# A graph, attention and gated-delta layer on one core: three sums leave TensorE, the gate projections move behind the others

## Chip, cores and metric

The kernel runs on 1 core of a Trainium2 chip (TRN2). The metric is the device time of one execution in microseconds (us). Engines are called PE (TensorE matmul), PEld (its weight load), DVE (VectorE), ACT (ScalarE), POOL (GpSimd) and SP (the engine that issues most DMAs).

## What is computed

One layer over 1250 nodes with 512 features, all in float32. Cut to what matters here:

```python
xn  = layernorm(x)
# graph convolution over 20000 edges plus self loops
deg = segment_sum(ones, dst_with_loops)          # edges into each node, plus 1
agg = segment_sum((xn @ W)[src] * (deg**-0.5)[src] * (deg**-0.5)[dst], dst)
# linear attention, 8 heads of 64
Q, K, V = elu(xn@Wq.T+bq)+1, elu(xn@Wk.T+bk)+1, xn@Wv.T+bv
mix = (Q @ (K^T V)) / (Q . K.sum(nodes) + 1e-6) @ Wo.T + bo
x   = x + relu(agg + b) + mix
# feed-forward: top-2 of 4 memories, gated delta rule, 8 heads of 64
h = layernorm(x)
q, k, v = l2norm(silu(h@Wq)), l2norm(silu(h@Wk)), silu(h@Wv)
beta, g = sigmoid(h@Wb), -exp(A_log)*softplus(h@Wa+dt_bias)
core = recurrence(q, k, v, beta, g)              # per memory and head
out  = x + (rmsnorm(core) * o_norm_weight * silu(h@Wg)) @ Wo
```

## The kernel before

Everything is scheduled by hand: each engine has one written list of instructions, and counting semaphores (`S[...]`) order the engines among themselves. An engine works strictly in the order of its list. Nodes are cut into NT = 10 tiles `t` of P = 125 rows; the 512 features into KC = 4 pieces `k` or `c` of 128. The stages, in the order of PE's list:

1. **Transposes** of the normalised rows into `xT`.
2. **Key and value stage** (PE lines L489 to L544). For each tile: four key matmuls (`project`, with the bias as a one-row matmul, L487), four value matmuls, and `kv_sums` (L538), which adds K^T V into PSUM bank 4 (L542) and the column sums of K into bank 5 with a column of ones (L544). From tile 2 on, 16 "sort steps" (L496) are put between them: small f16 matmuls that sort the edges into cells. DVE builds their one-hot operands in groups of four (`sort_four`, L1396 to L1400) and writes the finished key tile `tC` (L1413).
3. **Query and mixing stage** (L575, L596, L518, L520). `mix(t, b0)` makes one tile of the mixing output: a one-row bias matmul (L518) and four matmuls (L520). DVE adds the result to `x_all` (`mix_out`, L1441). Tiles 0 to 7 are made here, tiles 8 and 9 after the counting.
4. **Counting stage**. In NB = 20 groups `g` of SC = 9 steps, PE multiplies one-hot rows of sources with one-hot rows of destinations (`count_step`, L505), which gives the matrix `cnt` of edge counts; ACT copies it out of PSUM (L1020). DVE builds the one-hots: `oh_src` once a group (L1484), `oh_dst` once a step into WB = 4 buffers (L1488). Two of the matmuls of `xn @ W` (L653) stand in each group. POOL adds the unit matrix to the diagonal blocks of `cnt` (L1169), and after every second group PE sums the columns of the finished tile of `cnt` with ten one-column matmuls (`degrees`, L509 to L511). At the end DVE copies the degrees (L1530), POOL raises them to the power -0.5 (L1171, `dinv`), and DVE scales the rows `hs` (L1547).
5. **Aggregation** (L716): `cnt` times `hs`, 100 pairs.
6. **Feed-forward projections** (L748). `project_rows(t, w)` makes tile t of projection w (0 q, 1 k, 2 v, 3 gate), four matmuls each. ACT applies Silu (L1063, L1066). For q and k, DVE sums squares (`squares`, L1657), POOL takes the power (`inverse_norm`, L1185), DVE scales (`unit_rows`, L1665, L1667) and POOL scatters the finished row tile to `qkv_slots` in HBM with two indirect DMAs (`rows_out`, L1190). `gates_out` (L1180) scatters decays and betas; SP reads them back as `gbp`; `gates_in` on DVE orders them; `decay_sums` on PE (L760 to L767), `decays` on ACT (L1043) and `decay_rows` on DVE turn them into decay rows, which SP stores and loads again (L397, L404). SP then loads the sorted q and k rows (`load_qk`, L420).
7. **Chunk recurrence** in ten rounds: `features` transposes q and k (L794), `key_key` is the first of its products (L782), and so on.
8. **Output**: gather, norm, gate, last matmul (L958), store.

The order of the loops of stage 6, and where the decay work stands in them, is set by hand: by the loop over `w` and by `GAMMA_AT`. The code touched by the change:

## Time and profile before

| | before |
|---|---|
| median of 3 runs | 1128.72 us (1125.96 to 1130.7) |
| the profiled execution | 1125.21 us |
| its span | 1123.3 us |
| PE busy | 962.7 us (86%) |
| DVE busy | 598.7 us (53%) |
| POOL busy | 337.2 us (30%) |
| ACT busy | 249.0 us (22%) |
| mean granted TensorE clock | 0.948 of full speed |

The span is the stretch from the first to the last profiled instruction, and the execution's own time is 1.91 us more. Busy shares say which engine has most to do over the whole, not which one is waited for in a stage. The mean clock is that which the chip granted to PE over the span.

### The profile page before, as it was taken

The page shows a single profiled execution, that of the slowest core. Times are in us where ns is not written, and L with a number is a line of the kernel's source. Part 1 is how long each engine was busy: PE and PEld are TensorE (multiplying, and loading weights), DVE is VectorE, ACT ScalarE, POOL GpSimd, SP SyncE. Part 2 cuts the span into 40 slices and gives each one's busy share as a digit, 9 for nine tenths or more (in the row PEclk, how much of TensorE's full clock was granted, in tenths as well). Part 3 has the DMA queues.
Part 4 walks back from the last instruction along what each step waited for, and adds up shares of the span by engine and source line. Part 5 has one row for each costly group of instructions (what it writes and reads, how often), then busy time and mean ns, then how long its engine had stood idle before and what let it go on. Part 6 is the DMA issues. An engine that isn't in the chain of part 4 may idle for free.

```text
span 1123.3 us, 28924 instructions
## 1 busy us (share of the span) xinstructions
PE 962.7 (86%) x12841; PEld 620.7 (55%) x12841; DVE 598.7 (53%) x1297; ACT 249.0 (22%) x497; POOL 337.2 (30%) x284
## 2 busy tenths in 40 slices
PE   0899999999999989988999956878788987888468
PEld 0444444343777734434444426878778877788333
DVE  7878885333777522224533334555555644554265
ACT  0211112100111100003111113324423342233142
POOL 4000000000010000000585346554645464544282
PEclk9899999979999989998999987999999989999879
DMA  9100000000000041000044255443344334422252
GB/s 295 41 1 1 1 1 0 1 0 1 1 1 1 1 157 49 1 0 1 3 171 125 113 206 158 104 108 78 98 113 124 86 86 116 116 68 51 58 159 83
DMA packets 69982, 77.96 MB, mean 69 GB/s; under 512 B 33665, under 2 KB 55323, under 8 KB 69855
## 3 DMA queue, kind: packets, MB, share of 16 engines
q1 hardware_dynamic: 64735, 54.94, 18.1%
q0 software_dynamic: 5120, 21.14, 5.4%
q8 instruction: 103, 1.69, 0.6%
q14 instruction: 24, 0.20, 0.1%
HBM read 51.70 MB, written 24.35 MB: 68 GB/s over the span
## 4 chain that ended last, share of the span: by engine, by line
PE 80%; issue 6%; DVE 6%; ACT 3%; POOL 2%; DMA 1%; SPq 1%; ACTq 0%; DVEq 0%; POOLq 0%
PE bank L782 14%; PE bank L748 12%; PE bank L716 8%; PE bank L489 6%; PE bank L505 4%; PE bank L520 3%; PE bank L958 3%; PE bank L653 3%; PE bank L575 2%; PE bank L883 2%; PE bank L496 2%; PE bank L511 2%; PE bank L872 2%; PE bank L859 2%; PE bank L893 2%
## 5 line engine op out<-in xcount | busy, mean ns | idle before, releaser
L748 PE MATMUL bank<-W,xT 128*128 128x512 f32 x320 | 137.8, 593 | 0.0
L1169 POOL TENSOR_TENSOR big<-big,ident_sb 125x125 f32<-125x125 f32 x10 | 9.9, 989 | 346.2 <-ACT big L1020 346.2
L748 PEld LDWEIGHTS bank<-W,xT 128*128 128x128 f32 x320 | 60.6, 190 | 75.6 <-issue 75.6
L716 PE MATMUL bank<-hs,big 125*125 125x512 f32 x200 | 86.7, 593 | 1.3 <-DVE hs L1547 1.3
L1720 DVE TENSOR_TENSOR tB<-bank,masks_sb 128x512 f16<-128x512 f32 x80 | 52.7, 687 | 59.0 <-PE bank L782 58.8
L489 PE MATMUL bank<-W,xT 128*125 128x512 f32 x160 | 81.8, 610 | 0.0
L1488 DVE TENSOR_SCALAR rows<-iota_sb,tC 128x625 f16<-128x625 f16 x180 | 58.1, 383 | 30.6 <-PE bank L505 30.1
L782 PE MATMUL bank<-tB 64*64 64x64 f16 x2560 | 56.7, 200 | 15.7 <-issue 9.1
L505 PEld LDWEIGHTS bank<-rows 128*125 128x125 f16 x360 | 48.4, 144 | 31.2 <-issue 20.5
L505 PE MATMUL bank<-rows 128*125 128x313 f16 x360 | 62.4, 313 | 2.6 <-DVE rows L1488 2.4
L716 PEld LDWEIGHTS bank<-hs,big 125*125 125x125 f32 x200 | 37.2, 188 | 49.3 <-issue 48.5
L782 PEld LDWEIGHTS bank<-tB 64*64 64x64 f16 x2560 | 52.4, 116 | 19.0 <-issue 16.6
L782 PE MATMUL bank<-big 64*64 64x64 f32 x1920 | 59.1, 219 | 0.0
L782 PEld LDWEIGHTS bank<-big 64*64 64x64 f32 x1920 | 58.1, 135 | 0.3 <-issue 0.3
L1084 ACT ACTIVATE tA<-bank 128x512 f16<-128x512 f32 x60 | 36.0, 600 | 90.4 <-PE bank L782 90.3
L1220 POOL TENSOR_TENSOR big<-state,gtot 128x256 f32<-128x256 f32 x40 | 24.5, 612 | 101.0 <-DVE state L1748 101.0
L782 PE MATMUL bank<-tA 64*64 64x64 f16 x1280 | 34.1, 200 | 23.6 <-issue 20.5
L1398 DVE TENSOR_SCALAR rows<-iota_sb,gbp 125x180 f16<-125x180 f16 x160 | 51.5, 322 | 0.0
L1400 DVE TENSOR_SCALAR rows<-iota_sb,gbp 125x180 f16<-125x180 f16 x160 | 51.3, 321 | 0.0
L1162 POOL TENSOR_TENSOR rstd<-mv,phalf 125x5 f32<-125x5 f32 (+2 forms) x5 | 11.7, 2343 | 128.9 <-DVE mv L1316 128.9
L1227 POOL TENSOR_TENSOR tB<-tA,masks_sb 128x512 f16<-128x512 f16 x20 | 26.7, 1352 | 70.6 <-DVE tA L1705 70.6
L489 PEld LDWEIGHTS bank<-W,xT 128*125 128x125 f32 x160 | 28.0, 191 | 34.1 <-issue 34.1
(286 smaller groups left out, 1902.6 us busy)
## 6 DMA issues: line engine op xcount, KB each, us to landing
big<-qkv_slots SPq DMA_DIRECT2D x20, 512.0 KB, 5.4
rows<-step_rows SPq DMA_DIRECT2D x40, 128.0 KB, 3.8
rows<-gam_rows SPq DMA_DIRECT2D x40, 128.0 KB, 3.3
big<-qkv_slots SPq DMA_DIRECT2D x80, 64.0 KB, 3.9
big<-qkv_slots SPq DMA_DIRECT2D x40, 128.0 KB, 2.8
o_slots<-big SPq DMA_DIRECT2D x40, 128.0 KB, 2.4
x_all<-in_x SPq DMA_DIRECT2D x10, 224.0 KB
out<-tC SPq DMA_DIRECT2D x10, 224.0 KB
```

What stands on the lines that cost most here:

```text
L489: last = mm(dst, xT[:, k, t * P:(t + 1) * P], W[:, w, k, :], start=(k == 0 and bias is None), stop=(k == KC - 1))
L505: last = mm(bank[0:P, b0 + k, 0:n], oh_src[:, g % 2, j, 0:P], oh_dst[:, i % WB, t0:t0 + n], start=(j == 0), stop=(j == SC - 1))
L520: last = mm(bank[0:P, b0, :], qs[g % 2][:, c, at:at + P], W[:, 3, c, :], start=False, stop=(c == KC - 1))
L653: last = mm(bank[0:P, 6, :], xT[:, k, s * P:(s + 1) * P], W[:, 4, k, :], start=(k == 0), stop=(k == KC - 1))
L716: last = mm(bank[0:P, t % 2, :], cnt[:, s, t * P:(t + 1) * P], hs[:, s, :], start=(s == 0), stop=(s == NT - 1))
L748: last = mm(bank[:, 2 + w, :], xT[:, k, t * P:t * P + 128], W[:, w, k, :], start=(k == 0), stop=(k == KC - 1))
L782: last = mm(bank[q, b0, a * CL:(a + 1) * CL], lhsT[q, a, :], rhs[q, a, :], start=True, stop=True)
L1084: A(flat(T0[s] if lv == LEVELS - 1 else T16[s]), bank[:, TB[s], :], ACT.Copy).then_inc(S["t_done"], 1)
L1398: V.tensor_scalar(oh_col[:, i % (2 * SB), 0, :], iota[0:P, 0:SW], e_col[:, i:i + 1], e_src[:, i:i + 1], ALU.is_equal, ALU.mult)
L1400: V.tensor_scalar(oh_col[:, i % (2 * SB), 1, :], iota[0:P, 0:SW], e_col[:, i:i + 1], e_dst[:, i:i + 1], ALU.is_equal, ALU.mult).then_inc(S ...
L1488: V.tensor_scalar(oh_dst[:, i % WB, :], iota[:, 0:HN], srt[:, 1, i:i + 1], None, ALU.is_equal).then_inc(S["onehots_done"], 1)
L1720: V.tensor_tensor(B16[s], pm(MB[s]), bm(level[lv], 8), ALU.mult).then_inc(S["b_done"], 1)
```

## The change

Four things are changed, none of them in what is computed.

- **Mixing bias.** The one-row matmul L518 in `mix` goes. `bo` is loaded into all 125 rows, and POOL adds it to `x_all` ten times ahead of `mix_out`.
- **Key sums.** The ones-column matmul L544 goes from `kv_sums`. POOL adds the ten key tiles into `k_sum`; one ones-column matmul and four one-column matmuls on `k_sum` follow after the last `kv_sums`.
- **Degrees.** `oh_src` gets a 126th column of ones, so that row 125 of each product holds the counts per destination. Ten SP DMAs bring these rows to `deg_rows`, ten one-column matmuls turn them into columns, and DVE adds 1 for the loop. The 100 matmuls of `degrees` remain only in a branch for edge lists that need a second round. Edge destinations carry an offset of 1 so that empty places match no column. `mix(8)` and `mix(9)` now stand ahead of the degrees and the branch, and the feed-forward weights are loaded after `deg_psum`.
- **Gate projections.** `project_rows(t, 3)` moves behind all tiles of the other three; `project_rows(1, 0)` moves ahead of the routing matmuls; `decay_sums`, `decays` and `decay_rows` move up to tile 8, `gates_in` to tile 7, and DVE's `gate_rows` move behind the first `decay_matrix` pair.

```diff
@@ -49,7 +49,8 @@
 GB_FIRST = 4
-GAMMA_AT = 6
+GAMMA_AT = 7
+DECAY_AT = 8
@@ -147,7 +148,8 @@
         rows_all = sb("rows", [128, 6 * D])
-        b_o = xn[0:1, 0, :]
+        b_o = xn[0:P, 0, :]
+        k_sum = tA[0:P, 0, :]
@@ -172,6 +174,7 @@
+        deg_rows = W[0:NT, 1, :, :].rearrange("p k n -> p (k n)")[:, 0:N]
@@ -322,6 +325,14 @@
             return (LEVELS - 1) * (u - u % 2) + 2 * (lv - 1) + u % 2 + 1
+
+        def feature_count(t, w):
+
+            return 3 * NT + t + 1 if w == 3 else 3 * t + w + 1
+
+        def feature_bank(t, w):
+
+            return (5, 2, 3, 4)[t % 4] if w == 3 else 2 + w
@@ -373,8 +384,12 @@
             sp.wait_ge(S["kv_psum"], NT)
-            sp.dma_start(b_o, d["L0_mix_bo"].unsqueeze(0)).then_inc(S["bias_loaded"], 16)
+            sp.dma_start(b_o, d["L0_mix_bo"].partition_broadcast(P)).then_inc(S["bias_loaded"], 16)
+            for s in range(NT):
+                sp.wait_ge(S["count_done"], 2 * s + 2)
+                sp.dma_start(deg_rows[s:s + 1, :], big[P:OW, s * N:(s + 1) * N]).then_inc(S["deg_rows_loaded"], 16)
             sp.wait_ge(S["mix_psum"], NT)
+            sp.wait_ge(S["deg_psum"], 1)
@@ -502,7 +517,7 @@
                 for k, (t0, n) in enumerate(HCOLS):
-                    last = mm(bank[0:P, b0 + k, 0:n], oh_src[:, g % 2, j, 0:P], oh_dst[:, i % WB, t0:t0 + n],
+                    last = mm(bank[0:OW, b0 + k, 0:n], oh_src[:, g % 2, j, :], oh_dst[:, i % WB, t0:t0 + n],
@@ -515,9 +530,8 @@
                 at = (t - SEGS[g][0]) * P
-                mm(bank[0:P, b0, :], ones[0:1, 0:P], b_o, start=True, stop=False)
                 for c in range(KC):
-                    last = mm(bank[0:P, b0, :], qs[g % 2][:, c, at:at + P], W[:, 3, c, :], start=False, stop=(c == KC - 1))
+                    last = mm(bank[0:P, b0, :], qs[g % 2][:, c, at:at + P], W[:, 3, c, :], start=(c == 0), stop=(c == KC - 1))
@@ -532,17 +546,15 @@
             pe.wait_ge(S["off_done"], 2)
-            mm(bank[:, 5, :], zeros16[:, 0:128], zeros16[:, :], start=True, stop=True)
...
                 for c in range(KC):
-                    mm(bank[:, 4, c * 128:(c + 1) * 128], xn[0:P, t % 2, c * 128:(c + 1) * 128],
+                    last = mm(bank[:, 4, c * 128:(c + 1) * 128], xn[0:P, t % 2, c * 128:(c + 1) * 128],
                        tC[0:P, t % 2, c * 128:(c + 1) * 128], start=False, stop=True, skip_group_check=True)
-                mm(bank[0:1, 5, :], ones[0:P, 0:1], tC[0:P, t % 2, :], start=False, stop=True,
-                   skip_group_check=True).then_inc(S["kv_psum"], 1)
+                last.then_inc(S["kv_psum"], 1)
@@ -604,13 +616,16 @@
             kv_sums(NT - 1)
+            pe.wait_ge(S["pool_added"], NT - 1)
+            mm(bank[0:1, 5, :], ones[0:P, 0:1], k_sum, start=True, stop=True)
+            for c in range(KC):
+                last = mm(bank[:, 6, c:c + 1], k_sum[:, c * 128:(c + 1) * 128], ones[0:P, 0:1], start=True, stop=True)
+            last.then_inc(S["kv_psum"], 1)
...
             for c in range(KC):
-                mm(bank[:, 4, c * 128:(c + 1) * 128], b_v[:, c * 128:(c + 1) * 128], ks_row[:, c * 128:(c + 1) * 128],
+                last = mm(bank[:, 4, c * 128:(c + 1) * 128], b_v[:, c * 128:(c + 1) * 128], ks_row[:, c * 128:(c + 1) * 128],
                    start=False, stop=True, skip_group_check=True)
-            for c in range(KC):
-                last = mm(bank[:, 6, c:c + 1], ks_row[:, c * 128:(c + 1) * 128], ones[0:1, 0:1], start=True, stop=True)
@@ -653,11 +667,6 @@
                             last.then_inc(S["h_psum"], 1)
-                if g % 2 == 0 and g >= 2:
-                    pe.wait_ge(S["loops_added"], s)
-                    degrees(s - 1)
-            pe.wait_ge(S["loops_added"], NT)
-            degrees(NT - 1).then_inc(S["deg_psum"], 1)
@@ -678,22 +687,28 @@
+            pe.wait_ge(S["count_done"], NB)
+            for t in (8, 9):
+                mix(t, 2 + t % 2)
+            pe.wait_ge(S["h_done"], NT)
+            pe.wait_ge(S["deg_rows_loaded"], 16 * NT)
+            for t in range(NT):
+                last = mm(bank[0:P, 6, t:t + 1], deg_rows[:, t * P:(t + 1) * P], ones[0:NT, 0:1], start=True, stop=True)
+            last.then_inc(S["deg_psum"], 1)
+
             pe.wait_ge(S["rounds_done"], 1)
...
             with pe.If(n_rounds > 1):
-                pe.wait_ge(S["counted"], 1)
+                pe.wait_ge(S["mix_done"], NT)
                 with pe.Fori(1, n_rounds) as r:
...
                     count_round(r)
-                pe.wait_ge(S["counted"], 2)
+                pe.wait_ge(S["counted"], 1)
                 mm(bank[:, 7, 0:16], zeros16[:, 0:128], zeros16[:, 0:16], start=True, stop=True)
-            pe.wait_ge(S["count_done"], NB)
-            for t in (8, 9):
-                mix(t, 2 + t % 2)
             pe.wait_ge(S["h_done"], NT)
@@ -742,15 +757,21 @@
             def project_rows(t, w):
-                if t:
-                    pe.wait_ge(S["f_act"], 4 * (t - 1) + w + 1)
+                b0 = feature_bank(t, w)
+                if w < 3 and t:
+                    pe.wait_ge(S["f_act"], feature_count(t - 1, w))
+                if w == 3 and 1 <= t < 4:
+                    pe.wait_ge(S["f_act"], feature_count(NT - 1, t - 1))
+                if w == 3 and t >= 4:
+                    pe.wait_ge(S["f_act"], feature_count(t - 4, 3))
                 for k in range(KC):
-                    last = mm(bank[:, 2 + w, :], xT[:, k, t * P:t * P + 128], W[:, w, k, :], start=(k == 0), stop=(k == KC - 1))
+                    last = mm(bank[:, b0, :], xT[:, k, t * P:t * P + 128], W[:, w, k, :], start=(k == 0), stop=(k == KC - 1))
-            for w in range(4):
+            for w in range(3):
...
                 project_rows(0, w)
+            project_rows(1, 0)
@@ -767,9 +788,13 @@
             for t in range(1, NT):
-                for w in range(4):
+                for w in range(1 if t == 1 else 0, 3):
                     project_rows(t, w)
-            decay_sums()
+                if t == DECAY_AT:
+                    decay_sums()
+            pe.wait_ge(W_loaded[3], 32)
+            for t in range(NT):
+                project_rows(t, 3)
@@ -1163,6 +1196,14 @@
             rstd_of(2)
+            for t in range(1, NT):
+                pool.wait_ge(S["k_done"], t + 1)
+                if t >= 2:
+                    pool.wait_ge(S["pool_added"], t - 1)
+                G.tensor_tensor(k_sum, tC[0:P, 0, :] if t == 1 else k_sum, tC[0:P, t % 2, :], ALU.add).then_inc(S["pool_added"], 1)
+            pool.wait_ge(S["bias_loaded"], 32)
+            for t in range(NT):
+                G.tensor_tensor(x_all[:, t, :], x_all[:, t, :], b_o, ALU.add).then_inc(S["pool_added"], 1)
@@ -1334,11 +1375,11 @@
             step(V.tensor_scalar(e_int, e_int, 1, None, ALU.arith_shift_right))
-            step(V.tensor_copy(e_dst, e_int))
+            step(V.tensor_scalar(e_dst, e_int, 1.0, None, ALU.add))
...
             for b in range(NB):
-                step(V.tensor_scalar(binm[:, b, :], e_bin, float(b), None, ALU.is_equal))
+                step(V.tensor_scalar(binm[:, b, :], e_bin, float(b - 2), None, ALU.is_equal))
@@ -1410,6 +1451,7 @@
                     dve.wait_ge(S["kv_psum"], t - 1)
+                    dve.wait_ge(S["pool_added"], max(t - 2, 1))
@@ -1437,6 +1479,7 @@
             def mix_out(t, b0):
+                dve.wait_ge(S["pool_added"], NT + t)
@@ -1473,15 +1516,16 @@
                 dve.wait_ge(S["sort_used"], r * EPP + EPP)
-                V.tensor_scalar(srt[:, 0, :], bank[:, 7, 0:SW], -1.0, None, ALU.add).then_inc(S["sorted"], 1)
-                V.tensor_copy(srt[:, 1, :], bank[:, 7, SW:2 * SW]).then_inc(S["sorted"], 1)
+                V.tensor_scalar(srt[:, :, :], bank[:, 7, 0:2 * SW].rearrange("p (a n) -> p a n", a=2), -1.0, None,
+                                ALU.add).then_inc(S["sorted"], 1)
             keep_sorted(0)
-            dve.wait_ge(S["sorted"], 2)
+            dve.wait_ge(S["sorted"], 1)
+            V.memset(oh_src[:, :, :, P:OW], 1.0)
...
                     dve.wait_ge(S["onehots_used"], (g - 1) * SC)
-                V.tensor_tensor(oh_src[:, g % 2, :, :], bm(iota[:, 0:OW], SC), bc(srt[:, 0, g * SC:(g + 1) * SC], OW), ALU.is_equal)
+                V.tensor_tensor(oh_src[:, g % 2, :, 0:P], bm(iota[:, 0:P], SC), bc(srt[:, 0, g * SC:(g + 1) * SC], P), ALU.is_equal)
@@ -1526,8 +1570,10 @@
+            mix_out(8, 2)
+            mix_out(9, 3)
             dve.wait_ge(S["deg_psum"], 1)
-            V.tensor_copy(deg[:, :], bank[0:P, 7, 0:NT]).then_inc(S["counted"], 1)
+            step(V.tensor_scalar(deg[:, :], bank[0:P, 6, 0:NT], 1.0, None, ALU.add))
@@ -1538,8 +1584,6 @@
             V.tensor_copy(n_r, n_max).then_inc(S["deg_final"], 1)
-            mix_out(8, 2)
-            mix_out(9, 3)
@@ -1675,11 +1719,9 @@
                 unit_rows(t)
-                if t:
-                    gate_rows(t - 1)
...
                     gates_in()
-                if t == NT - 2:
+                if t == DECAY_AT:
@@ -1757,6 +1799,8 @@
             both(decay_matrix, 0)
+            for t in range(NT):
+                gate_rows(t)
```

Three places in the order of instructions (a row is source line, operation, output and inputs, shape, and how many in a row; the line numbers after the change are those of the new file, about 15 to 20 higher). First, PE in the middle of the counting stage, around the end of a second group, before:

```order
L653 MATMUL bank<-W,xT 125x512
L505 MATMUL bank<-rows 125x313
L505 MATMUL bank<-rows 125x312
L511 MATMUL bank<-ones,big 125x1 x10
L505 MATMUL bank<-rows 125x313
L505 MATMUL bank<-rows 125x312
```

and now:

```order
L667 MATMUL bank<-W,xT 125x512
L520 MATMUL bank<-rows 126x313
L520 MATMUL bank<-rows 126x312
L520 MATMUL bank<-rows 126x313
L520 MATMUL bank<-rows 126x312
L520 MATMUL bank<-rows 126x313
```

The ten one-column matmuls between two groups are gone, and a count matmul has 126 output rows in place of 125. Second, PE at the end of the counting, before (the branch body, which does not run with these inputs, is left out at the "..."):

```order
L505 MATMUL bank<-rows 125x313
L505 MATMUL bank<-rows 125x312
L511 MATMUL bank<-ones,big 125x1 x10
L682 TENSOR_LOAD rounds
...
L518 MATMUL bank<-xn,ones 125x512
L520 MATMUL bank<-W 125x512 x4
L518 MATMUL bank<-xn,ones 125x512
L520 MATMUL bank<-W 125x512 x4
L716 MATMUL bank<-hs,big 125x512 x60
```

and now:

```order
L520 MATMUL bank<-rows 126x313
L520 MATMUL bank<-rows 126x312
L534 MATMUL bank<-W 125x512 x8
L696 MATMUL bank<-ones,W 125x1 x10
L700 TENSOR_LOAD rounds
...
L731 MATMUL bank<-hs,big 125x512 x60
```

The last two mixing tiles moved ahead of the degrees, so the degrees, the register load and the branch now stand directly ahead of the aggregation. Third, PE in the feed-forward projections, before:

```order
L748 MATMUL bank<-W,xT 128x512 x16
L756 MATMUL bank<-sel,lt_sb 125x40
L757 MATMUL bank<-sel,onesq 125x40
L748 MATMUL bank<-W,xT 128x512 x144
L764 MATMUL bank<-ident_sb,gbg 128x64 x2
L764 MATMUL bank<-ident_sb,gbg 64x64
L766 MATMUL bank<-gbg,masks_sb 128x320
L767 MATMUL bank<-gbg,masks_sb 128x320
L794 MATMUL bank<-ident_sb,big 128x2x64 x16
```

and now:

```order
L768 MATMUL bank<-W,xT 128x512 x16
L777 MATMUL bank<-sel,lt_sb 125x40
L778 MATMUL bank<-sel,onesq 125x40
L768 MATMUL bank<-W,xT 128x512 x92
L785 MATMUL bank<-ident_sb,gbg 128x64 x2
L785 MATMUL bank<-ident_sb,gbg 64x64
L787 MATMUL bank<-gbg,masks_sb 128x320
L788 MATMUL bank<-gbg,masks_sb 128x320
L768 MATMUL bank<-W,xT 128x512 x52
L819 MATMUL bank<-ident_sb,big 128x2x64 x16
```

The decay matmuls moved 52 projection matmuls up: 12 of tile 9's q, k and v, and the 40 of the gate stand behind them.

## Rows read from the trace of the kernel before

**Rows 1.** The page, chain of work that ended last, share by engine.
```profile
PE 80%; issue 6%; DVE 6%; ACT 3%; POOL 2%; DMA 1%; SPq 1%; ACTq 0%; DVEq 0%; POOLq 0%
```

**Rows 2.** Windows: start:end length, busy per engine (PE first), PEclk, DMA share, GB/s.
```profile
318.00:322.00 4.00, 4.00 (x16) 2.74 (x15) 2.28 (x6) 0.00 (x0) 0.00 (x0) 0.62 0.02 4
560.00:600.00 40.00, 40.00 (x95) 17.76 (x94) 14.03 (x20) 6.88 (x12) 29.16 (x21) 1.00 0.41 160
```

**Rows 3.** Timeline of the key and value stage: start, length, engine, instruction [idle before].
```profile
109.22 1.02 PE L544 MATMUL bank<-tC,ones 125*1 125x512 f32 x2
110.09 0.32 DVE L1400 TENSOR_SCALAR rows<-iota_sb,gbp 125x180 f16<-125x180 f16 x1
...
110.89 1.12 PE L487 MATMUL bank<-big,ones 1*125 1x512 f32 x2
```

**Rows 4.** Timeline of the first mixing tile, PE's rows.
```profile
215.78 1.12 PE L518 MATMUL bank<-xn,ones 1*125 1x512 f32 x2
216.83 3.70 PE L520 MATMUL bank<-W 128*125 128x512 f32 x8
```

**Rows 5.** Timeline of two groups of the counting stage.
```profile
306.84 1.27 PE L505 MATMUL bank<-rows 128*125 128x313 f16 x8
...
311.35 1.27 PE L505 MATMUL bank<-rows 128*125 128x313 f16 x8 [0.18 <-DVE rows L1488]
...
315.52 2.24 PE L511 MATMUL bank<-ones,big 125*125 125x1 f32 x20
...
317.62 1.27 PE L505 MATMUL bank<-rows 128*125 128x313 f16 x8
```

**Rows 6.** Timeline of the counting's end, up to the aggregation.
```profile
389.55 0.77 ACT L1020 ACTIVATE big<-bank 125x313 f32<-125x313 f32 x2
390.39 0.41 POOL L1169 TENSOR_TENSOR big<-big,ident_sb 125x125 f32<-125x125 f32 x1 [9.50 <-ACT big L1020]
...
390.85 2.34 PE L511 MATMUL bank<-ones,big 125*125 125x1 f32 x20 [1.56 <-POOL big L1169]
...
394.98 1.96 POOL L1171 TENSOR_TENSOR dinv<-deg,phalf 125x10 f32<-125x10 f32 x1 [4.18 <-DVE t L1540]
...
395.82 2.07 PE L518 MATMUL bank<-xn,ones 1*125 1x512 f32 x2 [2.63 <-issue]
...
397.82 5.19 PE L520 MATMUL bank<-W 128*125 128x512 f32 x8
...
408.96 3.24 PE L716 MATMUL bank<-hs,big 125*125 125x512 f32 x7 [1.27 <-DVE hs L1547]
```

**Rows 7.** Timeline from the last projections to the first products.
```profile
655.84 0.60 ACT L1066 ACTIVATE big<-bank 128x512 f32<-128x512 f32 x1 [2.84 <-PE bank L748]
...
656.29 0.71 DVE L1667 TENSOR_TENSOR big<-big,nrm 128x512 f32<-128x512 f32 x1
...
659.17 0.39 PE L764 MATMUL bank<-ident_sb,gbg 64*128 64x64 f32 x3
659.27 0.60 ACT L1066 ACTIVATE hs<-bank 125x512 f32<-125x512 f32 x1 [2.84 <-PE bank L748]
...
660.13 0.70 PE L767 MATMUL bank<-gbg,masks_sb 128*128 128x320 f32 x2
...
665.98 0.95 POOL L1190 DMA_INDIRECT qkv_slots<-big,posi  x1 [0.30 <-issue]
...
677.72 3.59 PE L794 MATMUL bank<-ident_sb,big 128*128 128x128 f32 x16 [16.89 <-DMA big<-qkv_slots]
...
681.24 2.08 PE L782 MATMUL bank<-big 64*64 64x64 f32 x64
```

**Rows 8.** Chain of work, a later features pair: start, length, what.
```profile
703.00 1.90 PE bank L794 x16
```

**Rows 9.** Groups of instructions by form: count | busy us, mean ns | idle before.
```profile
L1231 POOL TENSOR_TENSOR xT<-xT,masks_sb 128x512 f32<-128x512 f32 x20 | 24.9, 1261 | 0.0
...
L1169 POOL TENSOR_TENSOR big<-big,ident_sb 125x125 f32<-125x125 f32 x10 | 9.9, 989 | 346.2 <-ACT big L1020 346.2
```

42 lines of the change are left out of this document (23 added, 19 removed).

## The prediction

> **What bounds the kernel now.** I read the chain of waits first: 80% of the chain that ended last is PE [rows 1]. So what counts is PE's own work in each stage and the places where PE stands still. Then I went through the timeline stage by stage, to see in each whether PE is waited for or waits. In the feed-forward projections PE is busy 40.00 of 40.00 us and POOL 29.16 [rows 2]. In the key and value stage PE has no gap of its own, but the sort steps after the key sum start when DVE's one-hots are ready [rows 3]. In the mixing tiles PE works through [rows 4]. In the counting PE and DVE nearly balance [rows 5]. Two places show PE standing: the counting's end, 2.63 us at the branch and 1.27 us for the scaled rows [rows 6], and the passage from projections to recurrence, 16.89 us for q and k rows on their way through HBM [rows 7].
>
> **Bias matmuls.** Each of the eight mixing tiles before the counting starts with L518; its four matmuls start 1.05 us behind it (216.83 less 215.78) and take 3.70 us [rows 4]. PE is not waited on by anyone else there, so 8 x 1.05 = 8.4 us go. Ten additions on POOL take their place, 1.26 us each by the nearest row of that size (L1231 [rows 9]), 12.6 us together. POOL has nothing else at that point of its list. Between the key stage and the first mixing tile PE makes nine query units of four matmuls, at the 3.43 us that four such matmuls take (655.84 to 659.27 [rows 7]) 31 us by estimate; even at 2.4 times the price, as L1169 stretches beside DVE (0.99 against 0.41 us [rows 6, 9]), the additions would be done in 30 us. If that cover were gone, each late addition would hold `mix_out` and, two tiles later, PE.
>
> **Key sums.** L544 holds PE 0.95 us of a tile. But the last one-hot that the four sort steps behind it need is only finished at 110.09 + 0.32 = 110.41, and the next key projection starts at 110.89 [rows 3]. Without L544 the fourth step can still not start before about 110.5, takes some 0.2 us, and the projection starts near 110.75: a gain of 0.15 us for each of eight tiles, 1.2 us, and 0.95 us for the first tile, which has no sort steps. The zeroing matmul of bank 5 gives 0.2 us. Bounds: 0.95 us for all nine (8.6 us) down to nothing; I take 2.3 us, since the DVE row decides. One key sum and four one-column matmuls remain at the end, as before. POOL's ninth addition has a query unit of 3.4 us and a `kv_sums` to finish in, for 1.26 us of work. The price of DVE and POOL disturbing each other is the first rival.
>
> **Degrees inside the counting.** From one group's start to the next is 4.51 us after a degree block (306.84 to 311.35), 4.17 us for PE's own work of the next group (311.35 to 315.52), and then ten one-column matmuls hold PE until 317.62 [rows 5]: 10.78 us a pair. The degree block is also the time in which DVE catches up, so a group without one keeps the small wait for DVE (0.18 us and its hand-over) and costs 4.51 us. A pair then takes 9.02 us, 1.76 us less, and there are nine such blocks inside the stage: 15.8 us. Bounds: 2.4 us a pair if DVE never delays PE (22 us in all), nothing if DVE should turn out the slower. A product of 126 rows in place of 125 has the same columns to stream, and I cost it at nothing.
>
> **The counting's end.** Counted from ACT's last copy (389.55), the aggregation starts at 408.96, 19.4 us later [rows 6]. Afterwards: copy 0.77 and hand-over 0.1; two mixing tiles without bias at 3.63 us pitch, 7.3; ten one-column matmuls as L511, 2.34; from the end of L511 (393.19) to POOL's power (394.98), 1.8, which holds DVE's copy and branch; the power, 1.96; scaling of the first rows with hand-over, 0.65. That is 14.9 us, 4.5 less. But PE now stands 4.4 us directly before the aggregation. Before, it stood 2.63 us, and the next work ran slow: 2.07 against 1.12 us for the bias and 5.19 against 3.70 us for the tile [rows 4, 6], 2.4 us in sum. I charge the aggregation the same 2.4 us and expect the mixing tiles, now 1 us behind the counting, to run at full rate. Net gain 2.1 us; bounds: 4.5, and minus 0.3 if both run slow. The last degree row's DMA must land within the 7.3 us of the mixing tiles. The nearest rows are the scatter and load of q and k rows, 11.7 us for two transfers one after the other (665.98 to 677.72 [rows 7]), so less than 6 us for one much larger: hidden. The feed-forward weights start some 8 us earlier than before and are hidden by the aggregation either way.
>
> **Gate projections behind the others.** Before, L748 ends at 659.17 and the first product of the recurrence (L782) starts at 681.24: 22.1 us. Afterwards the last q, k and v tile is done 34.3 us before the end of PE's projections (ten gate tiles at the 3.43 us between ACT's two copies, 655.84 and 659.27). The way of the last rows takes: from the copy of v to the end of unit_rows 1.2 us (656.29 + 0.71), then power, scatter, the load that ended at 677.72; even adding all of 659.17 to 677.72, 18.6 us, and 3.4 us because q and k now wait for one more stage of the decay rows, it fits in 34.3 us with 12 us over. POOL must keep up: 29.16 us of 40 for about four tiles [rows 2] are 7.3 us a tile and, with issue gaps, 8; the new pace of PE is 3 x 3.43 = 10.3 us. What PE pays: `decay_sums` themselves, 659.17 to 660.83, 1.7 us, now before the end of the projections; and a wait for `gates_in`, which follows DVE's unit_rows of tile 7. Unit_rows ends 1.2 us after ACT begins the copy of v, so gates_in with its two copies ends about 2 us after PE is free for `decay_sums`: 2 us of standing, bounds 0 and 5. Then 0.7 us for the last Silu, and 1.9 us for the features pair [rows 8], where it took 3.52 us before. 1.7 + 2.0 + 0.7 + 1.9 = 6.3, so 15.8 us are gained. The ten gate_rows on DVE lie under the gate projections; only the last ends about 1.4 us after PE, while PE is at the features. The extra changes of ACT's table delay no one, since PE needs the banks only three projections later.
>
> **Sum.** 8.4 + 2.3 + 15.8 + 2.1 + 15.8 = 44.4 us. From the profiled execution, 1125.2, that leaves 1080.8. It was 3.5 us under the median of the runs shown, 1128.7; against that the sum gives 1084.3. I predict 1083.
>
> **A rule against this change.** POOL stretches beside DVE: L1169 takes 0.41 us with DVE idle [rows 6] and 0.99 us in the mean [rows 9]; that DVE is held in turn, no row here shows plainly. The Trainium skill, SBUF — State Buffer, "Who interferes with whom", says that a DVE instruction with two SBUF inputs and a GpSimd instruction that reads SBUF exclude each other, and whichever starts second waits for the first to end. The stretched POOL row agrees. By that rule the key additions would hold DVE's L1396 as well, the first rival.
>
> **Rivals.**
> 1. *POOL's key additions hold DVE.* Each starts right behind the finished key tile, and DVE's next one-hots feed the steps which PE waits for [rows 3]. A hold of 0.5 us (the addition starts while DVE still waits for PE) costs 8 x 0.5 = 4 us, a full 1.26 us [rows 9] costs 10 us: 1087 to 1093. For it: POOL's stretching; against it: no lengthened DVE row. Chance 0.15.
> 2. *The counting does not speed up*, since DVE is the slower once PE's pauses are gone: for it, PE waits for DVE at the start of groups already; against it, 0.18 us is all [rows 5]. It gives 1083 + 15.8 = 1099. Chance 0.07.
> 3. *The rows come too late*: POOL, 8 us a tile against 10.3, catches up from its late start only slowly, or gates_in waits for the gates read back, and PE stands at `decay_sums` or at the features. It decides from 12 us of lateness; if all is lost, 1083 + 16 = 1099, with a wait of 5 us more 1088. Chance 0.08.
> 4. *The granted clock falls*: PE is denser. In one stretch of continuous work it had 0.62 [rows 2], in another 1.00. 1% of clock is some 9 us of PE work, so from 5% less in the mean the kernel is slower than before, about 1135. Against it: the densest stretch has 1.00. Chance 0.03.
>
> **How the numbers follow.** My sum has 0.67, with its own range 1075 to 1090. Rival 1 and the milder half of 3 take the range to 1095; the rest is left out. Range 1074 to 1095. Half a per cent, 5.6 us, is about what can be told from no change here. Every case but the last is faster by more than that: faster 0.96, same 0.01, slower 0.03.
>
> **What would show it.** Groups of the counting 4.5 us apart throughout; DVE's L1396 not lengthened or put off beside POOL's additions; PE at work from the last projection to the features with under 1.5 us of gap; a gap of about 2 us before `decay_sums`; 4 to 5 us of standing before the aggregation. I am wrong if pairs of groups stay near 10.8 us, if the tiles of the key stage get longer, or if PE waits for q and k rows after the gate tiles.

## The result and the profile after

The changed kernel takes 1085.82 us (median of 4 runs, 1082.52 to 1090.61); before it was 1127.34 us (4 runs, 1125.81 to 1130.7). The ratio is 0.9631, with a 95% interval from 0.9583 to 0.9679. The forecast was 1083, from 1074 to 1095. The profiled execution took 1088.01 us with a span of 1086.2, against 1125.21 and 1123.3 before. Every stage time below comes from one profiled execution of each kernel.

The total says nothing of the terms. Cut at the same instructions of PE in both traces, the stages show that four of them were 4 to 11 us off, two in each direction:

| stretch of the timeline | before | after | change | forecast |
|---|---|---|---|---|
| start to the first query matmul | 160.92 | 169.93 | +9.0 | -2.3 |
| on to the first mixing tile | 54.86 | 60.13 | +5.3 | 0 |
| on to the first counting matmul | 61.65 | 47.75 | -13.9 | -8.4 |
| on to ACT's last copy of the counts | 112.12 | 92.32 | -19.8 | -15.8 |
| on to the aggregation | 19.41 | 14.84 | -4.6 | -4.5 |
| aggregation and what follows, to the projections | 112.24 | 114.14 | +1.9 | +2.4 |
| projections, to the first product of the recurrence | 160.04 | 143.77 | -16.3 | -15.8 |
| recurrence and output | 442.1 | 443.3 | +1.3 | 0 |
| sum | 1123.3 | 1086.2 | -37.1 | -44.4 |

The page still shows PE as what bounds the kernel, but DVE has twice its share in the chain of work that ended last (section 4, the line that answers to [rows 1]):

```profile
PE 76%; DVE 12%; issue 7%; POOL 2%; ACT 2%; DMA 0%; SPq 0%; DVEq 0%; ACTq 0%; POOLq 0%
```

The largest loss is in the key stage. These rows of its timeline in the changed kernel answer to [rows 3] (start, length, engine, instruction, idle time before it and its releaser):

```profile
70.41 1.27 POOL L1203 TENSOR_TENSOR tA<-tA,tC 125x512 f32<-125x512 f32 x1 [9.19 <-DVE tC L1455]
...
71.20 1.02 DVE L1437 TENSOR_TENSOR rows<-iota_sb,gbp 125x512 f16<-125x512 f16 x1 [0.88 <-PE bank L511]
...
71.61 1.05 PE L555 MATMUL bank<-tC,xn 125*128 125x128 f32 x8
...
72.75 1.75 PE L511 MATMUL bank<-rows 125*128 125x360 f16 x4
...
74.43 1.12 PE L502 MATMUL bank<-big,ones 1*125 1x512 f32 x2
```

POOL's addition runs from 70.41 to 71.68, and DVE's first one-hot instruction, begun at 71.20, takes 1.02 us; free of POOL it takes 0.69. PE is through with the products at 72.66 and then spreads four sort steps over 1.75 us, since each needs a one-hot of its own. The clock is the other half of the picture. Windows of the key stage, of before and then of the changed kernel (PE busy first, PEclk is the granted clock as a share of 2.4 GHz):

```profile
60.00:160.00 100.00, 100.00 (x350) 44.08 (x348) 83.13 (x287) 14.59 (x24) 0.00 (x0) 1.00 0.00 1
```

```profile
60.00:160.00 100.00, 96.32 (x312) 43.26 (x311) 82.73 (x277) 13.36 (x22) 10.06 (x8) 0.93 0.00 0
```

PE stood 3.7 us of these 100, and its clock, which had never left 2.4 GHz here, fell to 1.2 GHz now and then. It can be seen in the same projection matmuls in two tiles, the second pair at nearly half the speed of the first:

```profile
108.75 1.02 PE L504 MATMUL bank<-W,xT 128*125 128x512 f32 x2
...
116.84 1.91 PE L504 MATMUL bank<-W,xT 128*125 128x512 f32 x2
```

The tiles are therefore of two kinds. From products to products they are 12.70 us apart at the higher clock and 14.4 where such a stretch lies in them, four of the seven full ones; before, all were 12.53 apart. In the mean, the groups of PE's instructions give 651 ns for one of the key and value projections,

```profile
L504 PE MATMUL bank<-W,xT 128*125 128x512 f32 x160 | 88.1, 651 | 0.0
L511 PE MATMUL bank<-rows 125*128 125x360 f16 x160 | 47.2, 327 | 7.6 <-DVE rows L1441 3.4
```

against 610 before (81.8 us in all, 6.3 less). Of the 9.0 us in the first row of the table, 8.0 lie between the products of tile 1 and the first query matmul (98.32 us, before 90.28). The other 1.0 lies ahead of that, where the first projections start at 43.78 in place of 42.05; among the kernels below that moment moves between 42.0 and 44.3 us, also where nothing ahead of it was edited.

In the query stage the bias additions meet DVE's next batch of one-hots:

```profile
178.86 1.42 DVE L1439 TENSOR_SCALAR rows<-iota_sb,gbp 125x180 f16<-125x180 f16 x1
...
178.91 13.02 POOL L1206 TENSOR_TENSOR x_all<-x_all,xn 125x512 f32<-125x512 f32 x10 [11.65 <-DMA xn<-in_L_mix_bo]
...
180.21 1.30 DVE L1441 TENSOR_SCALAR rows<-iota_sb,gbp 125x180 f16<-125x180 f16 x1
...
186.46 0.33 PE L511 MATMUL bank<-rows 125*128 125x360 f16 x1 [1.28 <-DVE rows L1441]
...
188.91 0.33 PE L511 MATMUL bank<-rows 125*128 125x360 f16 x1 [1.28 <-DVE rows L1441]
...
189.69 1.10 PE L636 MATMUL bank<-W,kvbd 128*128 128x512 f32 x2 [0.46 <-DVE tC L1497]
```

POOL's ten additions take 1.30 us each, and DVE's one-hots, otherwise 0.24 us apart, come one for each addition, 1.22 us apart. PE waits 1.28, 1.28 and 0.46 us for them. The forecast had charged these additions nothing. It asked whether POOL has the time, and not what DVE does beside them. These waits are 3.6 us of the stretch's 5.3 (24.22 us from the first query matmul to the fourth query unit, "unit 3" below, before 20.63); the other 1.7 are a stretch at the lower clock behind it, which other kernels below have as well (35.8 to 35.9 us from unit 3 to the first mixing tile, or 34.2 without it).

The counting went as forecast, its groups now 4.50 us apart throughout where [rows 5] have 10.78 for two:

```profile
302.55 1.27 PE L520 MATMUL bank<-rows 128*126 128x313 f16 x8 [0.16 <-DVE rows L1532]
...
307.05 1.27 PE L520 MATMUL bank<-rows 128*126 128x313 f16 x8 [0.17 <-DVE rows L1532]
```

The counting's end answers to [rows 6]:

```profile
370.13 0.77 ACT L1045 ACTIVATE big<-bank 126x313 f32<-126x313 f32 x2
370.92 0.70 SPq L390 DMA_DIRECT2D W<-big  x1
370.95 7.13 PE L534 MATMUL bank<-W 128*125 128x512 f32 x16 [1.08 <-ACT big L1045]
...
378.01 2.34 PE L696 MATMUL bank<-ones,W 10*125 10x1 f32 x20
...
382.33 1.97 POOL L1212 TENSOR_TENSOR dinv<-deg,phalf 125x10 f32<-125x10 f32 x1 [10.96 <-DVE t L1586]
...
384.97 2.04 PE L731 MATMUL bank<-hs,big 125*125 125x512 f32 x2 [4.62 <-DVE hs L1591]
```

From 370.13 to 384.97 are 14.84 us (14.9 forecast), with 4.62 us of standing (4.4). The passage to the recurrence answers to [rows 7]:

```profile
594.00 0.39 PE L785 MATMUL bank<-ident_sb,gbg 64*128 64x64 f32 x3 [1.48 <-DVE gbg L1677]
...
640.99 1.97 PE L819 MATMUL bank<-ident_sb,big 128*128 128x128 f32 x16 [0.69 <-ACT hs L1100]
642.88 1.32 PE L807 MATMUL bank<-big 64*64 64x64 f32 x38
```

The wait for `gates_in` is 1.48 us (2.0 forecast), the last Silu costs 0.69, and no wait for the q and k rows is left.

### The profile page after: what moved, and what is told of

Read it like the earlier page. It is cut to its first block, busy times and chain, and to the rows that moved or that the text cites. A ratio compares the mean times of both kernels' runs of the same rounds, so it can differ in the third digit from the quotient of the medians.

```text
span 1086.2 us, 28543 instructions
## 1 busy us (share of the span) xinstructions
PE 929.5 (86%) x12622; PEld 593.7 (55%) x12622; DVE 608.7 (56%) x1297; ACT 250.4 (23%) x498; POOL 365.5 (34%) x303
## 4 chain that ended last, share of the span: by engine, by line
PE 76%; DVE 12%; issue 7%; POOL 2%; ACT 2%; DMA 0%; SPq 0%; DVEq 0%; ACTq 0%; POOLq 0%
PE bank L807 15%; PE bank L768 12%; PE bank L731 8%; PE bank L504 7%; PE bank L983 3%; PE bank L534 3%; PE bank L520 3%; PE bank L908 2%; PE bank L897 2%; DVE rows L1528 2%; PE bank L587 2%; PE bank L918 2%; PE bank L922 2%; PE bank L884 2%; PE bank L667 2%
## 5 line engine op out<-in xcount | busy, mean ns | idle before, releaser
L504 PE MATMUL bank<-W,xT 128*125 128x512 f32 x160 | 88.1, 651 | 0.0
L1210 POOL TENSOR_TENSOR big<-big,ident_sb 125x125 f32<-125x125 f32 x10 | 11.4, 1143 | 168.0 <-ACT big L1045 168.0
L520 PEld LDWEIGHTS bank<-rows 128*126 128x126 f16 x360 | 45.0, 139 | 35.2 <-issue 24.3
L520 PE MATMUL bank<-rows 128*126 128x313 f16 x360 | 60.5, 305 | 4.4 <-DVE rows L1532 4.3
L1439 DVE TENSOR_SCALAR rows<-iota_sb,gbp 125x180 f16<-125x180 f16 x160 | 56.7, 355 | 0.0
L1441 DVE TENSOR_SCALAR rows<-iota_sb,gbp 125x180 f16<-125x180 f16 x160 | 54.5, 341 | 0.0
L511 PE MATMUL bank<-rows 125*128 125x360 f16 x160 | 47.2, 327 | 7.6 <-DVE rows L1441 3.4
```

The lines of the kernel that those rows point to most:

```text
L504: last = mm(dst, xT[:, k, t * P:(t + 1) * P], W[:, w, k, :], start=(k == 0 and bias is None), stop=(k == KC - 1))
L511: mm(bank[:, 7, 0:2 * SW], oh_row[:, i // SB % 2, i % SB, :], oh_col[:, i % (2 * SB), :, :].rearrange("p a n -> p (a n)"), start=False, st ...
L520: last = mm(bank[0:OW, b0 + k, 0:n], oh_src[:, g % 2, j, :], oh_dst[:, i % WB, t0:t0 + n], start=(j == 0), stop=(j == SC - 1))
L1439: V.tensor_scalar(oh_col[:, i % (2 * SB), 0, :], iota[0:P, 0:SW], e_col[:, i:i + 1], e_src[:, i:i + 1], ALU.is_equal, ALU.mult)
L1441: V.tensor_scalar(oh_col[:, i % (2 * SB), 1, :], iota[0:P, 0:SW], e_col[:, i:i + 1], e_dst[:, i:i + 1], ALU.is_equal, ALU.mult).then_inc(S ...
```

## The experiments

Ratios are against runs of the kernel before on the same chip. "Changed kernel" is the one of the diff, 1085.82 us; in its own comparison it stands at 0.9631.

**Gate projections back in their old place** (`for w in range(4)` in each tile, the decay sums behind all of them, ACT and DVE as before).

> The changed kernel with one part undone: the gate projections stand beside q, k and v of each tile again, and the decay work behind them. My theory: the wait of 16.9 us before the features comes back, and the 1.5 us wait for gates_in goes, so 15 to 17 us more than the changed kernel (about 1101 us). Rival (the gain at this place came from the granted clock or from other work): less than 8 us more.

Measured: 1107.31 us, ratio 0.9826 [0.9796, 0.9856], 21.5 us over the changed kernel. The trace is level with it up to the projections (498.88 against 499.11). Then PE waits for the q and k rows again:

```profile
655.85 1.94 PE L800 MATMUL bank<-ident_sb,big 128*128 128x128 f32 x8 [17.33 <-DMA big<-qkv_slots]
```

Its first product starts at 660.10, 17.2 us later than in the changed kernel, a little above the 15 to 17 expected; the total is further above them. The profiled spans are 19.9 us apart: 2.2 us of the other 2.7 arise in the recurrence, where this run changes only the place of DVE's `gate_rows`. It starts there at the lower clock, behind the wait (its first 64 products take 2.83 us, 2.08 in the changed kernel); what makes the rest was not looked into.

**Degrees back in the counting** (`degrees(s - 1)` inside every second group, no column of ones, mixing tiles 8 and 9 behind the branch).

> The changed kernel with the degrees summed on PE inside the counting again. My theory: a pair of groups takes 10.8 us again in place of 9.0, nine times, and the counting's end 19 in place of 15 us, against which the aggregation starts at full clock (2 us back): 17 to 19 us more than the changed kernel (about 1103 us). Rival (part of the 20 us that the counting lost in the profile is clock dips): 10 to 15 us more.

Measured: 1108.54 us, ratio 0.9831 [0.9805, 0.9857], 22.7 us over the changed kernel, above both expectations. Up to ACT's last copy of the counts it is 20.4 us behind (390.64 less 277.91, against 92.32). The nine pauses of 1.76 us (10.78 us less twice 4.51, [rows 5]) are only 15.8 of that. The rest can be seen in the timeline of before, where PE runs at its lower clock behind some of the degree blocks, as here behind the one of [rows 5], with nearly twice the 1.24 us of a usual group:

```profile
320.22 2.28 PE L505 MATMUL bank<-rows 128*125 128x313 f16 x8
```

In the changed kernel no group from 298 us on is above 1.27 us.

**Key sums back on TensorE** (GpSimd's nine key additions gone, the matmul against a column of ones in each tile again).

```
                 mm(bank[:, 4, ...], xn[...], tC[...], start=False, stop=True, ...)
+                mm(bank[0:1, 5, :], ones[0:P, 0:1], tC[0:P, t % 2, :], start=False, stop=True, ...)
```

> The changed kernel with the key sums on PE again, no key additions on POOL. Theory of the lock: each POOL addition holds DVE's first one-hot instruction behind it for 0.33 us (1.02 in place of 0.69 us), which takes back most of the 0.15 us of gain per tile: the kernel is within 2 us of the changed one, and the tiles of the key stage are 12.5 us apart at full clock in place of 12.7. Rival (POOL's additions cost nothing, the key stage lost time to the clock alone): 2 to 4 us more than the changed kernel.

Measured: 1071.23 us, ratio 0.9507 [0.9477, 0.9538], 14.6 us under the changed kernel. Both theories fell. The same moment as in the changed kernel's key stage above reads:

```profile
73.22 1.05 PE L556 MATMUL bank<-tC,xn 125*128 125x128 f32 x8
...
74.20 1.02 PE L558 MATMUL bank<-tC,ones 125*1 125x512 f32 x2
...
75.16 0.79 PE L511 MATMUL bank<-rows 125*128 125x360 f16 x4
```

From the start of the products to the end of the four sort steps it takes 2.73 us with the key sum and 2.89 without. The 1.0 us of key sum had filled a wait for DVE. Between 60 and 160 us PE is busy 100.00 us at a clock of 1.00, and the tiles are 12.53 us apart again. The first query matmul starts at 163.50 in place of 169.93, although the products of tile 1 start 1.6 us later (73.22, not 71.61): the key stage itself is 8.0 us shorter.

**Bias matmuls back** (`mm(bank[0:P, b0, :], ones[0:1, 0:P], b_o, start=True, stop=False)` ahead of each mixing tile, no bias additions).

> The changed kernel with the mixing bias as a one-row matmul on PE again, no bias additions on POOL. Theory of the lock: ten matmul pairs of 1.05 us come back, but the eight DVE one-hots of 1.23 us start to start return to 0.24 us, which gives PE 3.5 us back: 6 to 8 us more than the changed kernel. Rival (DVE's long rows are hidden and cost PE nothing): 10.5 us more.

Measured: 1095.25 us, ratio 0.9726 [0.9695, 0.9757], 9.4 us over the changed kernel, between the two expectations. Both effects are there. From the first query matmul to unit 3 it needs 20.81 us, as before (20.63), where the changed kernel needs 24.22: the additions' hold costs 3.4 us. This is not a fixed price: the kernels with early bias additions and without key sums on PE need from 24.2 to 28.2 us here, among them the run with ten matmuls at the head, which edits nothing in this stage, 26.79. And each mixing tile has its bias matmul again, a pitch of 4.68 us against 3.46. At the first transposes of the recurrence it is 12.7 us behind the changed kernel; the recurrence gives 5 us back.

**Key sums on TensorE and the additions on GpSimd too.** That left two causes for the 14.6 us: the additions that hold DVE, or the matmuls that PE no longer has. This kernel has both, with nobody reading GpSimd's sum.

> The key sums are on TensorE again as in the run with the key sums back, and GpSimd makes its eight key additions beside them all the same (nobody reads their sum). Theory gaps (the addition holds VectorE's one-hots by 0.33 us a tile, TensorE stands for them, and the standing brings the granted clock down): the last one-hot of the four comes 0.33 us later than in that run, TensorE stands some 0.4 us a tile, the clock of 60 to 160 us falls below 1.00 in part, and the time is 1074 to 1081. Rival (the key sum matmuls that are gone from TensorE's stream are what the clock misses, and the additions cost next to nothing): 1071 to 1073, TensorE busy without a gap and the clock 1.00 between 60 and 160 us.

Measured: 1070.62 us, ratio 0.9512 [0.9468, 0.9557], the same as without the additions. Window:

```profile
60.00:160.00 100.00, 100.00 (x344) 43.39 (x344) 85.20 (x286) 14.68 (x25) 10.02 (x8) 1.00 0.00 0
```

My theory fell, the rival held: PE has no gap and the clock stays at 1.00. The hold itself is still there (DVE's first one-hot takes 1.01 us), but PE comes to the sort steps 1 us later and meets little of it: the tiles are 12.69 us apart, 0.16 more than without the additions, 1.3 us over the stage. The first query matmul starts at 162.76.

**No key additions at all, no key sums either** (the additions for tiles 0 to 7 are left out).

> The changed kernel without the key additions of tiles 0 to 7: GpSimd adds once, for the last two tiles, so the key sums of the others are left out of the output. Neither a key sum matmul nor a held one-hot in tiles 1 to 8. If the hold is the cause of the 15 us: the one-hots come 0.33 us a tile sooner than in the changed kernel, and the time is that of the run with the key sums back less up to 2.3 us, 1068 to 1071, clock 1.00. If any standing at the sort steps costs the clock (there are still some 0.7 us a tile, since the four one-hots take VectorE longer than TensorE needs for the products of keys and values): 1077 to 1085, clock 0.93 to 0.96 between 60 and 160 us.

Measured: 1079.66 us, ratio 0.9574 [0.9529, 0.9619]. There is less work on PE and on GpSimd than in the run before, and it takes 9 us more. Four of the seven full tiles are 12.37 us apart, 0.16 less than with the key sums, as the forecast had it; the other three take 14.06, with a stretch at the lower clock. So the missing key sums lose 4.1 us in the key stage, without one addition on POOL (94.37 us against 90.28). The first query matmul starts at 164.03, against 163.50 with the key sums, whose stage began later. PE stands 2.6 us of the window, and the clock is lower:

```profile
60.00:160.00 100.00, 97.39 (x318) 43.67 (x318) 81.02 (x279) 13.99 (x23) 0.00 (x0) 0.95 0.00 0
```

Behind it, against the run before, 3.5 us go where the bias additions hold the batch that PE needs next (24.21 us from the first query matmul to unit 3, against 20.71), and 5.0 in the recurrence.

**Key additions later** (each waits until DVE has built its tile's last one-hot).

```
                 pool.wait_ge(S["k_done"], t + 1)
+                if t >= SORT_FROM:
+                    pool.wait_ge(S["sort_oh"], SORT_KV * (t - SORT_FROM) + SORT_KV)
```

> The changed kernel with each key addition started behind VectorE's last one-hot of its tile, some 4 us later, when the batch that TensorE waits for next is built. Theory hold: no one-hot that TensorE waits for is held, so the time is that of the run without key additions within 1 us. If any standing costs the clock, it is 1077 to 1085 as there. Rival (the additions hurt wherever they lie, since VectorE is busy 83 of 100 us here): 1084 to 1087 as the changed kernel.

Measured: 1084.15 us, ratio 0.9635 [0.959, 0.968]. The key stage is that of the run without additions (busy 97.37, clock 0.95, 94.08 us long against 94.37), so it doesn't matter that DVE is held at another time. Of the 6.3 us won up to the first query matmul (163.63), 2.4 are gone at unit 3, which comes 26.65 us behind it (24.22 in the changed kernel). The total doesn't tell this run from the changed kernel and lies in the rival's range, but what the rival says of the key stage is not so.

**Key sums back, bias additions late, decay sums one tile later.**

```
             pool.wait_ge(S["bias_loaded"], 32)
+            pool.wait_ge(S["sort_oh"], EPP)
...
-DECAY_AT = 8
+DECAY_AT = 9
```

> The changed kernel with the key sums back on TensorE, GpSimd's bias additions started only when VectorE has built its last sort one-hot, and the decay sums behind the ninth tile of projections in place of the eighth. Theory: the ten bias additions hold no one-hot any more, which gives back what TensorE stands for them (some 5 us with the pace after it), the decay sums 0 to 1.5 us: 1064 to 1067. Rival (VectorE's other work between 200 and 215 us is held instead, the scaling of the queries, for which TensorE waits as well): 1069 to 1073.

Measured: 1069.16 us, ratio 0.9497 [0.9458, 0.9537], not told apart from the key sums back alone, and above the 1064 to 1067 of the theory. There was nothing to give back: with the key sums on PE, unit 3 comes 20.63 us behind the first query matmul even with the additions early, because they meet a batch that PE needs only later.

**Zeros in the place of the key sums.**

```
                 last.then_inc(S["kv_psum"], 1)
+                for n in range(4):
+                    mm(bank[:, 5, :], zeros16[:, 0:128], zeros16[:, :], start=True, stop=True)
```

> The changed kernel with four matmuls of zeros (float16, 128 by 512) behind each tile's products of keys and values, where the sum over the tile's keys stood; nobody reads their result. Theory gaps (what TensorE lost with the key sums is its cover while VectorE builds the one-hots: it stands, and the granted clock falls): TensorE busy without a gap and the clock 1.00 between 60 and 160 us, the first query matmul at 163 to 164 us in place of 169.93, and the time 1072 to 1080, by where the recurrence's code comes to lie. Rival (the real key matmuls matter in another way, for instance through the banks that they touch or the float32 rows that they stream): the clock stays at 0.93 to 0.96 there, and the time 1084 to 1088.

Measured: 1088.73 us, ratio 0.966 [0.9621, 0.9698]. The key stage did what the gap theory says, the total did not:

```profile
60.00:160.00 100.00, 98.97 (x361) 46.05 (x360) 86.00 (x286) 14.59 (x24) 9.93 (x9) 1.00 0.00 0
```

The seven full tiles are all 12.69 or 12.70 us apart, and the first query matmul starts at 163.86, 6.1 us sooner than in the changed kernel. Unit 3 then comes 28.20 us behind it, 4.0 later than there. Up to the recurrence 3.8 us are left, and the recurrence then takes 5.5 us longer.

**Ten small matmuls at the head of PE's stream**, to find what moves the recurrence.

```
+            for n in range(10):
+                mm(bank[:, 5, 0:16], zeros16[:, 0:128], zeros16[:, 0:16], start=True, stop=True)
             for t in range(LB):
                 transpose_row(0, t)
```

> The changed kernel with ten matmuls of 16 columns of zeros at the head of TensorE's stream, where it stands some 30 us for the first normalised rows, and nothing else. The runs with 10 more TensorE instructions ahead of the recurrence than the changed kernel (key sums back, bias back, both) needed 391 to 392 us from the first transposes of the recurrence to those of the output stage, the changed kernel and those with its count 396 to 398, all at the same granted clock, with 41 us of TensorE's idle time there put down to issue against 54. Theory place (where the recurrence's instructions lie in the stream decides it): about 392 us there, and the time 1079 to 1081. Rival (it comes from the key sums, or by chance): 396 to 398 us there, and the time 1084 to 1087.

Measured: 1082.84 us, ratio 0.962 [0.9581, 0.9659]. As a total that can't be told from the changed kernel. In the trace, the recurrence begins at 640.04 (640.99 in the changed kernel) and the output stage's transposes, PE's first work behind it, stand 7.2 us apart. First this run, then the changed kernel:

```profile
1032.03 1.90 PE L976 MATMUL bank<-ident_sb,big 125*128 125x125 f32 x8 [20.96 <-DVE big L1841]
```

```profile
1039.19 1.90 PE L974 MATMUL bank<-ident_sb,big 125*128 125x125 f32 x8 [21.09 <-DVE big L1839]
```

**Zeros ahead of the aggregation** (the kernel with the late bias additions, and twice six matmuls of zeros where PE stands 4.6 us), and **twelve at the head** of the same kernel instead.

> The kernel with the key sums back, the bias additions late and the decay sums later, and two times six matmuls of zeros between the degree matmuls and the aggregation, where TensorE stands 4.6 us and the aggregation starts at the lower clock. Theory: the aggregation's first groups run at the higher clock, 2 us less: 1066 to 1068. Rival (the zeros delay the wait for the scaled rows, or the clock is low there for another reason): 1069 to 1071.

> The kernel with the key sums back, the bias additions late and the decay sums later, and twelve matmuls of 16 columns of zeros at the head of TensorE's stream, where it stands for the first rows: as many instructions more than in that kernel as the run with the zeros ahead of the aggregation had, but none of them near work that sets the end. Theory place: the recurrence takes about 401 us from its first transposes to those of the output stage in place of 391.7, and the time is 1077 to 1080. Rival (the zeros ahead of the aggregation had cost what that run lost): 391 to 393 us there, and the time 1068 to 1071.

Measured: 1077.61 us, ratio 0.9559 [0.9521, 0.9596], and 1073.45 us, ratio 0.9547 [0.9523, 0.9571]. The first is 8.5 us above the kernel with the late bias additions, and above both expectations. The profiled executions stand further apart, 14.0 us. About 1.5 us of that are the zeros' own: the second six start after 2.20 us of issue time, run at the lower clock and end 2 us after DVE has begun to scale the rows:

```profile
374.79 2.72 PE L717 MATMUL bank<-zeros 125*128 125x512 f16 x6 [2.20 <-issue]
377.30 18.00 PE L735 MATMUL bank<-hs,big 125*125 125x512 f32 x39
```

The aggregation's first 5 us then ran at a clock of 0.78 in place of 0.59, but up to the projections the stretch was not shorter (115.3 us against 114.2). In the recurrence lie 9.6 us, and the second run has 7.9 of them, without a zero anywhere near. Its time was still below the 1077 to 1080 that I expected: its first query matmul starts at 159.34 against 162.93, and it reaches the recurrence 5.6 us sooner. That the zeros at the head did this is not shown. The first projections start 2.0 us sooner than in the kernel with the late bias additions (42.16 against 44.20), but kernels with no zeros at the head have that as well (42.05 before the change, 42.01 without key additions), and the ten of the run before brought 1.7 us at the first query matmul, as the run with the bias back had without them (168.28 and 168.32).

The key stage in all the traces, from the products of tile 1 to the first query matmul, with the distance of its seven full tiles and the clock between 60 and 160 us:

| kernels | length | tiles apart | clock |
|---|---|---|---|
| before; key sums back; bias late; zeros ahead of the aggregation; twelve at the head | 90.28 | 12.53 | 1.00 |
| key sums on both; zeros in the key stage | 91.58 | 12.69 | 1.00 |
| no key additions; key additions late | 94.37; 94.08 | 12.37, three 14.06 | 0.95 |
| changed; gates, degrees or bias back; ten at the head | 98.3 | 12.70, four 14.4 | 0.93 |

All kernels, from the first transposes of the recurrence to those of the output stage (the instructions counted are matmul calls that stand ahead of the recurrence in the program, against the changed kernel):

| kernel | calls | first transposes | length |
|---|---|---|---|
| changed | 0 | 640.99 | 398.2 |
| no key additions | 0 | 635.09 | 397.3 |
| key additions late | 0 | 635.15 | 397.0 |
| key sums back | +10 | 631.65 | 391.6 |
| bias back | +10 | 653.68 | 393.2 |
| key sums on both | +10 | 629.84 | 392.3 |
| bias late | +10 | 628.93 | 391.7 |
| ten at the head | +10 | 640.04 | 392.0 |
| zeros ahead of the aggregation | +22 | 632.94 | 401.3 |
| twelve at the head | +22 | 623.29 | 399.6 |
| zeros in the key stage | +40 | 637.17 | 403.7 |
| degrees back | +90 | 664.50 | 396.4 |
| before | +110 | 677.72 | 399.4 |
| gate projections back | 0 | 655.85 | 402.8 |

In the first eleven rows the lengths fall into groups by the count, whatever the added calls do and wherever they stand. The last row doesn't fit its count. It and the kernel before begin the recurrence behind the wait for the q and k rows and take 4.25 and 3.52 us to the first product, the others 1.9; counted from there, the row has 398.6 us against 395.1 to 396.3 for the three others with its count, so 2.2 us or more stay unexplained. The counts 40, 90 and 110 have no second kernel to compare with. Two pairs differ in the calls at the head alone: ten at the head against the changed kernel (392.0 and 398.2) and twelve at the head against the bias late (399.6 and 391.7). Their medians, 3.0 and 4.3 us apart in the same directions, have intervals that overlap. And each length is that of one execution, while executions of one kernel lie up to 10 us apart (no key additions, 1072.75 to 1082.32 us). The clock doesn't go with the length: 0.95 in the changed kernel's recurrence and 0.95 in the one with ten at the head. PE's idle time put down to issue is 53.8 us in the changed kernel, 47.9 with ten at the head, 41.0 with the key sums back and 57.6 with the zeros in the key stage.

## Why the forecast was right, and where it wasn't

**The total** was right within 3 us, in part by luck: the forecast was 11.3 and 5.3 us too good for the two stretches up to the first mixing tile, and 5.5 and 4.0 us too bad for the mixing tiles and the counting, and these errors largely cancel. The profiled executions stand 37.2 us apart and the medians 41.5, for a sum of 44.4.

**Key sums (2.3 us forecast).** The forecast read rightly that DVE's last one-hot sets the end of the four sort steps: where the clock holds and nothing holds DVE, a tile gains 0.16 us (12.37 in place of 12.53), and 0.15 had been forecast. Two things were left out of the sum. The step that failed most is that it took standing in place of working as free. Without additions, or with late ones, the key stage has a stretch at the lower clock in three tiles, some 1.7 us each, and is 4.1 and 3.8 us longer than before. The other is "the price of DVE and POOL disturbing each other is the first rival": the additions alone, with the key sums kept, add 1.3 us. Both together, as in the changed kernel, cost 8.0 us: 1.3 for the hold and 6.7 for four stretches at the lower clock. Zeros in the key sums' place, with the additions as they were, give the 6.7 us back, and the clock of 1.00 with them; so it is PE's being busy in that wait that counts, not what the matmuls computed. The Trainium skill, TensorE: Matmul & The Clock Gate, "What's actually happening", says that the clock is granted by how busy the engine has been; these windows agree (1.00 with 100.00 and 98.97 us busy of 100, 0.95 with 97.4, 0.93 with 96.3). The forecast had the clock as its fourth rival, but from PE being denser. It fell with PE less dense.

**The first rival** is thus right in its mechanism, and so is what the prediction took for it from the Trainium skill, SBUF — State Buffer, "Who interferes with whom", on a DVE instruction with two SBUF inputs: 1.02 us in place of 0.69 for the first one-hot instruction, L1437. The one-hots held in the query stage, one for each addition, have one SBUF input, so that they are held is shown by the trace and not foretold by that sentence. The rival's price of 4 to 10 us was too high for the hold, which is 0.33 us a tile against a tile with neither key sum nor addition and 1.3 us over the stage against before. That the stage lost 8.0 us comes from the clock, and the same thing happens without the rival.

**Bias (8.4 us).** Each tile lost 1.22 us rather than 1.05, 9.6 in all between the first tile's start and the last one's end; 4.3 us more came from the query work between the two sets of four tiles, where the execution before ran at a mean clock of 0.52 from 240 to 249 us and the changed one, from 244 to 258, at 0.92. Where such stretches fall moves from kernel to kernel, but the kernels with the bias matmuls have more of them: from the first mixing tile to the first counting matmul they take 61.65 and 64.94 us (bias back), the twelve without 47.75, four of them up to 2.7 more. Against it stand 3.4 us for the additions in the query units, which the forecast charged nothing since POOL had the time; the run without them doesn't have this wait, and the runs with them have 3.4 to 7.4 us or nothing, by where DVE's batch and PE meet them.

**Degrees in the counting (15.8 us).** The pace is exact, 4.50 us a group. The 4 us on top go with the stretches at the lower clock that stand behind some of the degree blocks; they come with the blocks, since from the first counting matmul to ACT's last copy the two kernels with blocks take 112.1 and 112.7 us and the twelve without 92.1 to 92.3. What in a block brings the clock down was not tested.

**The counting's end (2.1 us)** came to 2.7: 4.6 gained, 1.9 lost behind the standing, where the aggregation's first 5 us run at a clock of 0.60, before 1.00. The forecast charged 2.4 for it. Filling that wait with zeros didn't pay.

**Gate projections (15.8 us)** gave 16.3; `gates_in` is 0.5 us sooner than costed. With the decay sums one tile later the stretch takes 142.2 us in place of 143.8, in each of the three kernels that have them there.

**The recurrence**, which the forecast left alone, takes between 391.6 and 403.7 us from kernel to kernel. That the place of its code in PE's stream decides this fits eleven of the fourteen rows and both pairs in which nothing else was edited; it is not shown, with one execution for each length, one row against it and two that can't tell. What in the chip would do it (how code is brought in, how it is aligned) no run here shows. So of the 16.1 us between the profiled spans of the changed kernel and the one with the key sums back, 8.0 arise in the key stage less 1.6 for its later start, 2.6 in the query and mixing stages, 0.3 up to the first transposes of the recurrence, and 6.6 in the recurrence, whose cause is open.

The kernel with the key sums back on PE and the other three parts as changed is the fastest shown, 1069 to 1071 us, 0.95 of before. The zeros at the head together with another ten or so calls more or less, to find a better place for the recurrence, were not tried.
